# A CIN tower and its top network: sums over the embedding dimension moved from VectorE to ScalarE, top network cut into matmuls with 64 outputs

## The reference

```python
e = stack([tbl_f[ids[:, f]] for f in range(32)], axis=1)        # 1024 x 32 x 16
xk = x0 = e
for W in (W0, W1, W2):
    xk = relu(einsum('bmd,bhd,mhk->bkd', x0, xk, W))              # 1024 x 64 x 16
    outs.append(sum(xk, axis=2))                                  # 1024 x 64
h = concatenate([outs[0], outs[1], outs[2], dense_ctx], axis=1)   # 1024 x 208
h = maximum(h @ W_top1 + b_top1, 0)                               # 512 wide
h = maximum(h @ W_top2 + b_top2, 0)                               # 256 wide
y = h @ W_top3                                                    # 1024 x 1
```

## Time and profile before

| | |
|---|---|
| median of 3 executions | 626.93 us (626.72 to 628.49) |
| the profiled execution | 622.48 us, span on the core 620.7 us |
| mean granted TensorE clock | 0.991 |
| PE busy | 563.6 us, 91% of the span |
| DVE busy | 546.5 us, 88% |
| POOL busy | 488.3 us, 79% |
| ACT busy | 308.2 us, 50% |
| traffic | 150.89 MB, 243 GB/s |

### The profile page before, as it was taken

The page is one execution under the profiler, slowest core; times in us unless marked ns, Lnnn a source line. Parts: engine busy times, 40 slices in busy tenths (PEclk is TensorE's granted clock), DMA queues, the critical chain, the costliest instruction groups (busy, mean ns, idle before and its releaser), DMA issues.

```text
span 620.7 us, 7817 instructions
## 1 busy us (share of the span) xinstructions
PE 563.6 (91%) x2548; PEld 194.8 (31%) x2548; DVE 546.5 (88%) x321; ACT 308.2 (50%) x1345; POOL 488.3 (79%) x364
## 2 busy tenths in 40 slices
PE   0058997999999999999999999999999999999997
PEld 0012232332322333333333333333333333334354
DVE  0038997999999999999999999999999999999580
ACT  0023735355464745455476736454565736454442
POOL 6765888887889798988888788988888797949360
PEclk9997999999999999999999999999999999999998
DMA  3198878778586868788686858787776858687000
GB/s 99 29 375 315 309 249 310 274 267 295 191 314 210 316 218 311 270 299 295 223 289 215 310 199 313 261 310 274 251 275 213 289 212 311 255 306 271 2 1 0
DMA packets 52852, 150.89 MB, mean 243 GB/s; under 512 B 9830, under 2 KB 17386, under 8 KB 52810
## 3 DMA queue, kind: packets, MB, share of 16 engines
q1 hardware_dynamic: 44608, 148.27, 65.6%
q0 software_dynamic: 8192, 2.11, 2.5%
q10 hardware_dynamic: 10, 0.00, 0.0%
HBM read 147.20 MB, written 3.15 MB: 242 GB/s over the span
## 4 chain that ended last, share of the span: by engine, by line
DVE 33%; PE 29%; DMA 19%; issue 8%; POOL 8%; SPq 2%; ACT 1%; DVEq 0%; POOLq 0%
DVE prod L336 31%; PE y_ps L518 26%; DMA x0bc<-x_rows 14%; POOL emb L291 6%; DMA emb<-table,row_sb 2%; DVE z L364 2%; DMA x_rows<-emb 2%; PE x0g_ps L579 2%; POOL pool_prod L306 2%; SPq L263 1%; PE x0g_ps L584 1%; PE x0g_ps L602 0%; SPq L236 0%; SPq L246 0%; DMA off_sb<-id_offset 0%
## 5 line engine op out<-in xcount | busy, mean ns | idle before, releaser
L336 DVE TENSOR_TENSOR prod<-x0bc,x_ps 128x2048 f32<-128x2048 f32 (+1 forms) x252 | 456.5, 1887 | 13.6 <-ACT x_ps L418 13.1
L518 PE MATMUL y_ps<-prod,w_sb 128*64 128x512 f32 x1640 | 381.2, 598 | 12.2 <-DVE prod L336 12.0
L291 POOL DMA_INDIRECT emb<-table,row_sb x256 | 244.9, 957 | 65.5 <-issue 62.8
L306 POOL TENSOR_TENSOR pool_prod<-x0bc,x_sb 128x1024 f32<-128x1024 f32 x102 | 242.4, 2384 | 48.1 <-ACT x_sb L435 35.0
L518 PEld LDWEIGHTS y_ps<-prod,w_sb 128*64 128x64 f32 x1640 | 115.5, 137 | 253.4 <-issue 214.0
L425 ACT ACTIVATE relu<-y_ps 128x16 f32<-128x16 f32 x480 | 79.6, 296 | 115.3 <-PE y_ps L518 115.3
L418 ACT ACTIVATE x_ps<-y_ps 64x512 f32<-64x512 f32 x128 | 73.0, 570 | 75.4 <-PE y_ps L518 72.8
L518 PE MATMUL y_ps<-pool_prod,w_sb 128*64 128x512 f32 x408 | 104.9, 594 | 2.1 <-POOL pool_prod L306 2.0
L336 DVE TENSOR_TENSOR prod<-x0bc,x0g_ps 128x2048 f32<-128x2048 f32 x32 | 72.8, 2288 | 37.5 <-DMA x0bc<-x_rows 32.4
L435 ACT ACTIVATE x_sb<-relu 64x512 f32<-64x512 f32 x128 | 80.4, 628 | 3.4
L425 ACT ACTIVATION_READ_ACCUMULATOR relu<-y_ps 128x1 f32 x480 | 79.7, 322 | 0.0
(11 more groups left out here) (34 smaller groups left out, 71.0 us busy)
## 6 DMA issues: line engine op xcount, KB each, us to landing
x0bc<-x_rows SPq DMA_DIRECT2D x256, 512.0 KB, 7.0
x0g<-x_rows SPq DMA_DIRECT2D x16, 512.0 KB, 4.7
emb<-table,row_sb POOLq DMA_INDIRECT x256
x_rows<-emb SPq DMA_DIRECT2D x16, 128.0 KB, 2.1
w_sb<-w SPq DMA_DIRECT2D x2, 512.0 KB, 4.7
x_rows<-emb SPq DMA_DIRECT2D x16, 64.0 KB, 2.0
wt_sb<-wt SPq DMA_DIRECT2D x1, 512.0 KB
wt1a_sb<-wt_a SPq DMA_DIRECT2D x1, 256.0 KB
```

The lines of the kernel that those rows point to most:

```text
L291: pool.indirect_dma_start(emb[:, turn, DIM * n:DIM * (n + 1)], None, table, bass.IndirectOffsetOnAxis(row_sb[:, at:at + 1], 0)).then_inc(g ...
L306: pool.tensor_tensor(pool_prod[:, n % POOL_RING, 0:width(s)], x0bc[:, slot(s, j), 0:width(s)], x[:, 0:width(s)], ALU.mult).then_inc(pool_p ...
L336: made = dve.tensor_tensor(out, left, right, ALU.mult)
L518: made = pe.matmul(ps[MAPS * h:MAPS * (h + 1), 0:half(s)], w, moving[:, half(s) * h:half(s) * (h + 1)], start=first, stop=final)
```

## The change

1. `sums(s, 0)` for all steps and `sums(s, 1)` for all but the last go from VectorE to ScalarE: 32 ACTIVATEs of 16 columns, from `relu` in SBUF to a tile `spare`, each with an accumulated sum. `sums(s, 0)` stands between `square(s + 1)` and `finish(s, 1)`, `sums(s, 1)` behind `finish(s + 1, 0)` and the pieces of the top network. VectorE keeps the two last sums.
2. Every matmul of the top network with 128 outputs becomes two of 64 outputs (`by_halves`). THIRD now has the hidden rows as the weights and `W_top3` as the one moving column, so that the output comes as columns on up to 128 partitions, and each chunk stores one or two such columns.
3. Runs of like ACTIVATEs send one signal, at the last (L418, L425, L435 of before).
4. The loads of the top network's weights go from behind the tiles of step 1 to behind the tiles of step 3 on SP's queue. The store and the `x0g` load of the next step are now issued at the end of `load_tiles`, so the weights come behind the `x0g` load of step 4 and ahead of its tiles. `AHEAD` is empty and `GATHERED_FIRST` is 2, so these two new settings move nothing else.
5. The signals of the tiles are split by even and odd steps.

```diff
+def outputs_before(s):
+    return sum(columns_out(c) for i in range(s) for c, piece in PIECES.get(i, []) if piece == THIRD)
...
             def load_tiles(s):
-                for j in range(TILES):
+                store_at, load_at = AHEAD.get(s, (TILES, TILES))
+                for j in range(TILES + 1):
+                    if s + 1 < STEPS:
+                        if j == store_at:
+                            store_rows(s + 1)
+                        if j == load_at:
+                            load_x0g(s + 1)
+                    if j == TILES:
+                        break
...
-                if s == 1:
+                if s == 3:
                     for dst, src in ((wt1a_sb[:], wt1_a), (wt1b_sb[:], wt1_b), (wt2_sb[:], wt2), (wt3_sb[:], wt3),
...
                 layer(s, 1, x1_ps)
                 if s < LAST:
                     layer0(s + 1)
-                sums(s, 0)
                 layer(s, 2, x2_ps)
-                sums(s, 1)
-            sums(LAST, 2)
+            last_sums(1)
+            last_sums(2)
             last_input()
...
+            def sums(s, l):
+
+                act.wait_ge(relu_done[l], s + 1)
+                if l == 1 or s > 0:
+                    act.wait_ge(act_summed[1 - l], s + l)
+                for b in range(ROWS_OF[s] // 2):
+                    cols, at = slice(DIM * b, DIM * (b + 1)), FIRST_ROW[s] // 2 + b
+                    made = act.activation(spare[:, cols], relu[:, l, cols], ACT.Copy, accum_out=z[:, l, at:at + 1])
+                made.then_inc(act_summed[l], 1)
...
                     place_x0g(s + 1)
                     square(s + 1)
+                sums(s, 0)
                 finish(s, 1, x2_ps, x2_sb)
                 if s < LAST:
                     finish(s + 1, 0, x1_ps, x1_sb)
                 for c, piece in PIECES.get(s, []):
-                    take(c, piece)
+                    if piece != THIRD:
+                        take(c, piece)
+                if s < LAST:
+                    sums(s, 1)
+                for c, piece in PIECES.get(s, []):
+                    if piece == THIRD:
+                        take(c, piece)
...
+            def by_halves(ps, w, moving, first, final):
+
+                for h in range(2):
+                    made = pe.matmul(ps[MAPS * h:MAPS * (h + 1)], w[:, MAPS * h:MAPS * (h + 1)], moving, start=first,
+                                     stop=final)
+                return made
+
+            def third(c, ps):
+
+                for b in range(0, CHUNK_ROWS[c], MAPS):
+                    half_of = slice(b % P, b % P + MAPS)
+                    for k in range(H2_TILES):
+                        made = pe.matmul(ps[half_of, b // P:b // P + 1], h2[:, k, b:b + MAPS], wt3_sb[:, k:k + 1],
+                                         start=k == 0, stop=k == H2_TILES - 1)
+                return made
```

More of the change, by code:

```diff
@@ L51 @@
 GATHERS_AFTER = {1: [1, 1, 8], 2: [1, 1, 4]}
+GATHERED_FIRST = 2
+AHEAD = {}
 def columns(s):
@@ L129, with copies_after, columns_out @@
 SIGNALS_OF_CHUNK = 5
-PIECES_OF_CHUNK = H1_TILES + H2_TILES + 1
+PIECES_OF_CHUNK = H1_TILES + H2_TILES
 def taken_before(s):
-    return sum(2 if piece in (FIRST_A, FIRST_B) else 1 for i in range(s) for _, piece in PIECES.get(i, []))
-def summed2_after(s):
-    return FIRST_ROW[min(s + 1, LAST)] // 2 + (1 if s == LAST else 0)
+    return sum(2 if piece in (FIRST_A, FIRST_B) else 1 for i in range(s) for _, piece in PIECES.get(i, [])
+               if piece != THIRD)
+def copies_after(s, l):
+    return sum(1 for i in range(s + 1) if pool_tiles(i, l + 1))
+def columns_out(c):
+    return -(-CHUNK_ROWS[c] // P)
+def outputs_before(s):
+    return sum(columns_out(c) for i in range(s) for c, piece in PIECES.get(i, []) if piece == THIRD)
 def slot(s, j):
@@ L205, in cin_tower_kernel @@
         x0g_in = sem("x0g_in")
-        bc_in = [sem(f"bc_in{g}") for g in range(TILES // GROUP)]
+        bc_in = [[sem(f"bc_in{i}_{g}") for g in range(TILES // GROUP)] for i in range(2)]
         w0_ready = sem("w0_ready")
@@ L278, in _ @@
                         sp.dma_start(dst, src).then_inc(mlp_in, 16)
-            sp.wait_ge(stored, 16 * len(CHUNKS))
+            sp.wait_ge(stored, 16 * sum(map(columns_out, range(len(CHUNKS)))))
         @block.gpsimd
@@ L318, in _ @@
             pool.wait_ge(rows_done, 2)
-            gather(1, 0, GATHERS_OF[1])
+            for s in range(1, GATHERED_FIRST):
+                gather(s, 0, GATHERS_OF[s])
             pool.wait_ge(w0_ready, 2)
@@ L468, in output @@
                 if c > 0:
-                    act.wait_ge(stored, 16 * c)
-                act.activation(y_sb[:, 0:n], ps, ACT.Copy).then_inc(mlp_act, 1)
-                act.wait_ge(mlp_act, PIECES_OF_CHUNK * (c + 1))
-                act.dma_start(out[first:first + n, :].rearrange("b o -> o b"), y_sb[:, 0:n]).then_inc(stored, 16)
+                    act.wait_ge(stored, 16 * sum(map(columns_out, range(c))))
+                for col in range(columns_out(c)):
+                    rows = min(P, n - P * col)
+                    act.activation(y_sb[0:rows, col:col + 1], ps[0:rows, col:col + 1], ACT.Copy).then_inc(y_ready, 1)
+                act.wait_ge(y_ready, sum(map(columns_out, range(c + 1))))
+                for col in range(columns_out(c)):
+                    rows = min(P, n - P * col)
+                    act.dma_start(out[first + P * col:first + P * col + rows, :], y_sb[0:rows, col:col + 1]
+                                  ).then_inc(stored, 16)
             def take(c, piece):
@@ L483, in take @@
                 else:
-                    output(c, piece + 1, x0g_ps[0:1, 1, 0:n])
+                    output(c, piece + 1, x0g_ps[:, 1, :])
             def last_chunk():
```

109 lines of the change are left out of this document (54 added, 55 removed).

## The result

The changed kernel takes 736.50 us (median of 4 runs, 733.75 to 738.93), the kernel before 627.71 us beside it (4 runs, 626.72 to 629.23): a ratio of 1.173, with an interval of 1.168 to 1.178. The forecast was 648.6 us, at most 668. The sign was right, the size was not: +109 us where +22 were forecast. The profiled execution has a span of 735.2 us.

A forecast was written before the change was run, and what follows sets the result against it. VectorE paced the 34.34 us step; a 30.7 us loop through ScalarE would take over with a pass. 21.3 - 1.4 + 1.5 + 0.3 = +21.7 us on 626.9 gave 648.6 us, range 631 to 668.

The forecast's parts named there:

- What bounds the kernel: VectorE sets the 34.34 us step; a 30.7 us loop through ScalarE, POOL, SP becomes 35.8 us with a pass and leads.
- the named signs: Profile after: steps about 35.8 us, ScalarE's PE waits under 20 us, POOL and VectorE waiting, passes of 5.0 to 5.4 us.
- `sums(s, 0)`: On ScalarE's loop before layer 1's `finish`: 5.1 us a pass, 15 x 5.1 - 55.2 = +21.3 us.
- my upper bound: Layer 0's pass on ScalarE: at most 6.35 us, 0.198 us a pair reading SBUF, giving +40.1 us.
- The slack of 55.2 us: ScalarE before layer 1's `finish`: 15 waits for PE, 55.2 us in total, which the passes eat first.
- The end, -1.4 us: Behind the `finish` at 553.44, PE will have caught up: -1.4 us, between 0 and -4.2.
- `sums(s, 1)`, cost 0: On ScalarE ahead of its wait for layer 2, longer than a pass in nearly all steps: cost 0.
- VectorE's relief worth nothing: VectorE and PE then wait some 1.6 to 2.7 us in every step, so their relief gains nothing.
- The output as columns, +0.3 us: Top network's output: columns lengthen only the last store, +0.3 us, between 0 and 1.
- Weights behind step 3, +1.5 us: SP's queue: seven weight loads ahead of step 4's tiles cost +1.5 us once, between 0 and 4.8.
- 64 outputs a matmul, 0, and one signal a run, 0: Top network on PE: two halves cost one full matmul, 0, +6 at most; waiters always needed a run's last, 0.
- Dearer pairs "beyond 6.35 us": Rival on layer 0's pass: SBUF makes pairs dearer, beyond 6.35 us a pass; 668 us and more, chance 0.06.

The follow-up runs named there:

- g_none: Changed kernel with one gather a step in place of 16 from step 2 on: 619.09 us; the kernel before, cut likewise: 620.02 us.
- g_mix: Changed kernel with gathers behind layer 1's products dealt 4, 4, 2 in place of 1, 1, 8: 717.79 us; the kernel before, dealt likewise: 708.97 us.
- wide: Changed kernel with layer 0's pass as nine copies of 512 columns and one of 8, its sums left out: 663.76 us, 1.051 of the kernel before.
- s1dve: Changed kernel with the sums of layer 1 back on VectorE, those of layer 0 still on ScalarE: 739.16 us, 1.173 of the kernel before.
- best1: Changed kernel with layer 0's sums back on VectorE, output as a row, weights at step 1: 627.24 us, 0.993 of the kernel before.
- m_row: Changed kernel with both sums back on VectorE, output as a row, weights at step 1: 627.46 us, 0.994 of the kernel before.
- row_w3: Changed kernel with both sums back on VectorE and output as a row, weights still behind step 3: 629.23 us, 1.000 of the kernel before.

## Why the prediction was wrong

*What bounds the kernel.* Right. The loop through `x2_sb`, GpSimd's layer 2 and gathers, the store, `x0g` and ScalarE took over, and these of the named signs appeared: ScalarE's waits for PE gone, POOL's for `x_sb` and VectorE's for `x_ps` in every step. Its length without the pass was forecast as 30.7 us and measured as 30.4 to 31.3. The signs that hang on the price of a pass did not appear: steps of some 43 us and not 35.8, passes of 9.2 to 13.0 and not 5.0 to 5.4, ScalarE busy 67% more and not 50%. VectorE's busy time fell by 15.0 us, not 20. Two slips in the sums change nothing: the copy and the squares take 2.01 us and not 2.05, and the end at its better bound takes off 2.8 us and not 2.6.

*`sums(s, 0)`: this step failed.* The form of the sum held, its price didn't. I took 5.1 us a pass from the 32 pairs of layer 2, between 4.1 and 6.35. Two things were wrong with it. First, undisturbed passes take 6.45 us, a pair 0.20 us (6.35 us to the start of the next instruction): my upper bound, worked out from the dearer instructions that read SBUF, was the right value, and I chose the row of the same form over it. That is 15 x 6.45 - 55.2 = +41.6 in place of +21.3. Second, and larger, a pass at this place takes 9.2 to 13.0 us. The 15 passes add up to 169.0 us, 169.0 - 55.2 = +113.8, against +108.8 measured. What held them up (g_none, g_mix) is GpSimd's row of eight gathers behind layer 1. I had followed only the gathers of layer 2, as work on the loop, and had not asked what the others do to the stretch in which the pass would run. The step that failed is a duration read from one place and used at another.

The Trainium skill's budget of about 0.3 us an ACTIVATE with a bias operand (ScalarE: Activation LUTs, Rules for kernel authors) gave a pass of 10 us and +94 us, much nearer to the result than my sum; I had given such a price no chance of its own. The runs don't bear out its price all the same: pairs of two instructions come every 0.20 us in 17 of 31 passes here and in all of them without the gathers. It came near by a coincidence of sizes.

*The slack of 55.2 us.* About right. The `finish` of layer 1 of step 14 started at 553.44 us before, and in the changed kernel and in wide:

```profile
668.51 2.34 ACT L445 ACTIVATE x_ps<-y_ps 64x512 f32<-64x512 f32 x4
```

```profile
594.61 2.34 ACT L447 ACTIVATE x_ps<-y_ps 64x512 f32<-64x512 f32 x4
```

That is 115.1 us later, where the measured passes less the slack give 113.8, and 41.2 us later, where 15 x 6.06 - 55.2 = 35.7. Both traces also have two steps behind an output that are some 5 us longer than the others (wide: 41.6 and 42.2 beside 36.7), so the waits left out some 5 to 8 us of room. Traces have to be compared with traces here: the profiled execution of the kernel before is 5.2 us faster than the median beside the change.

*The end, -1.4 us.* The sign was right: from that `finish` to the end of the span are 66.7 us, before the change 67.3. Since 5.3 us of the 66.7 belong to the output's last store, the end itself became some 6 us shorter, a little beyond my bound of -4.2.

*`sums(s, 1)`, cost 0.* Right (s1dve; best1 against m_row).

*VectorE's relief worth nothing.* Right (the same two comparisons).

*The output as columns, +0.3 us.* Wrong by its size: 14.5 us. I priced the last store alone, and that too low (5.3 us), and not the gathers in flight behind the two outputs that come while there are still gathers. I had counted its instructions and not its packets.

*Weights behind step 3, +1.5 us.* Within its bounds; row_w3 can't tell it from zero.

*64 outputs a matmul, 0, and one signal a run, 0.* Together they gain 0.6% (m_row, interval 0.2% to 0.9%), which I had not expected. Layer 2's pass took 5.40 us before and 5.37 after, so the signals of that pass give little; the two were not separated.

*The rivals.* Dearer pairs "beyond 6.35 us" had 0.06 and 668 us and more. It was the nearest one, but as a matter of SBUF; a pass stretched by another engine was not among them.

## What to carry to other kernels

A price read from a row of the same form holds for the place where that row ran. Before dense small instructions are moved, look at what the other engines do in the stretch they move to, GpSimd's gathers first; here nine calls of 512 columns and one of 8 took such a place unharmed where 32 of 16 columns with a sum each didn't. And when an output is cut into narrow pieces, count its packets: here their cost appeared in the gathers that were waited for next.

## What the runs showed of the hardware

A row of GpSimd's gathers without other work between them holds up ScalarE's instructions. Alone, small instructions start 0.10 us apart; beside such a row one to four of them come every 0.7 us, sometimes 1.4, from some 23 to 47 instructions into the pass until typically 1.6 to 1.9 us after the last gather. With a product of 2.4 us between groups of at most four gathers the gaps are 6.5 us in place of 58.3. Ten long instructions in the same stretch are not held up (wide, 6.06 us of work in 6.06 us). The profile shows no releaser for it and calls it issue. The Trainium skill (Runtime: NRT & Kernel Launch, Instruction fetch mechanics) says that instructions are fetched ahead and that this is hidden. If the gaps are fetches, the trace disagrees with it by 58.3 us; whether it is the fetch that stalls here, or the sequencer, stays open. The DMA queues of the changed kernel within the gaps, 236.6 to 243.1 us, hold only these two, and none of those that the page calls "instruction":

```profile
q1 hardware_dynamic: 475, 1.70, 70.1%
q0 software_dynamic: 230, 0.06, 5.3%
```

So no block of instructions landed in the gaps of this pass. In nine of the 14 passes with gaps one does (of q14 in seven, of q8 in two), as in those between 192.7 and 200.5 us, where the same view also has:

```profile
q14 instruction: 1, 0.01, 0.3%
```

The gaps go on behind it, and they look the same in the five passes that have none. So neither a landing nor its absence goes with them. Which engine a block is for the view doesn't say. By what path the gathers reach ScalarE, no run here can tell.
